# A two-branch FFN kernel on one core: its first products and first coefficient in another order

## The reference, cut to what matters

```
xn = layernorm(x)
s  = attn_ref(xn)      # 4-bit weights (16 levels x block scales) with low-rank parts, gate/up/down with silu
g  = silu(ffn_ref(xn)) # the branch below
x + s * g

# ffn_ref, HID 512, INTER 1792, three weights (w1 gate, w3 up, w2 down), each with its mean_w:
def _binary_diff_weight(w, base):
    d = w - base
    coeff = mean(abs(d))
    return base + coeff * sign(d)
h = silu(xn @ W1.T) * (xn @ W3.T);  out = h @ W2.T
```

## Time and profile before

| | |
|---|---|
| median of 3 runs | 534.47 us (534.46 to 535.68) |
| the profiled execution | 534.48 us, its span 532.7 us |
| PE busy | 519.8 us, 98% of the span, 2352 matmuls |
| DVE busy | 443.0 us, 83% |
| ACT busy | 328.5 us, 62% |
| POOL busy | 94.6 us, 18% |
| chain that ended last | PE 95%, DVE 3%, DMA 1% |
| granted PE clock | 0.999 of full |

### The profile page before, as it was taken

The page is one execution under the profiler, slowest core; times in us unless marked ns, Lnnn a source line. Parts: engine busy times, 40 slices in busy tenths (PEclk is TensorE's granted clock), DMA queues, the critical chain, the costliest instruction groups (busy, mean ns, idle before and its releaser), DMA issues.

```text
span 532.7 us, 6530 instructions
## 1 busy us (share of the span) xinstructions
PE 519.8 (98%) x2352; PEld 432.1 (81%) x2352; DVE 443.0 (83%) x520; ACT 328.5 (62%) x455; POOL 94.6 (18%) x106
## 2 busy tenths in 40 slices
PE   4999999999999999999999999999999999999997
PEld 3778888888888888888888888888888888888886
DVE  6989998988896988865898888999999898874447
ACT  2979978557546655446648557968776585464310
POOL 1311002003100310022003121300310040004491
PEclk9999999999999999999999999999999999999999
DMA  8999905045711491059228994941592387127503
GB/s 337 394 401 404 385 8 168 15 137 98 197 54 46 76 234 49 1 106 223 56 70 160 250 217 90 186 101 40 109 187 47 74 163 144 36 46 161 135 20 139
DMA packets 31745, 76.73 MB, mean 144 GB/s; under 512 B 3873, under 2 KB 7297, under 8 KB 31585
## 3 DMA queue, kind: packets, MB, share of 16 engines
q1 hardware_dynamic: 21632, 57.42, 34.4%
q0 software_dynamic: 9792, 18.88, 20.5%
q10 hardware_dynamic: 288, 0.02, 0.0%
HBM read 53.23 MB, written 2.10 MB: 104 GB/s over the span
## 4 chain that ended last, share of the span: by engine, by line
PE 95%; DVE 3%; DMA 1%; issue 0%; ACT 0%; SPq 0%
PE up_ps L1726 28%; PE gate_pair L1726 27%; PE down_pair L1767 11%; PE up_ps L1767 9%; PE down_ps L1767 7%; PE side_ps L1810 2%; PE down_pair L1726 2%; PE down_pair L1677 1%; PE up_ps L1887 1%; PE gate_pair L1887 1%; PE down_pair L1887 1%; DMA xn<-in_x 1%; PE down_pair L1849 1%; PE gate_pair L1767 1%; PE down_pair L1782 1%; DVE xn L1135 1%
## 5 line engine op out<-in xcount | busy, mean ns | idle before, releaser
L1726 PE MATMUL up_ps<-xT,gu 128*128 128x512 f32 x648 | 151.9, 390 | 0.0
L1726 PE MATMUL gate_pair<-xT,gu 128*128 128x512 f32 x624 | 148.4, 390 | 0.9 <-DVE gu L1175 0.9
L1726 PEld LDWEIGHTS up_ps<-xT,gu 128*128 128x128 f32 x648 | 121.6, 188 | 25.1
L1726 PEld LDWEIGHTS gate_pair<-xT,gu 128*128 128x128 f32 x624 | 117.2, 188 | 25.4 <-DVE gu L1175 1.4
L655 POOL DMA_DIRECT2D y<-y_part x64 | 55.4, 878 | 338.3 <-ACT y_part L819 337.1
L806 ACT ACTIVATE h<-up_ps 128x512 fp32r<-128x512 f32 x52 | 31.1, 597 | 110.1 <-DVE up_ps L1242 57.0
L865 ACT ACTIVATE ramp<-codes,bend_bias 128x1536 f32<-128x1536 uint8 x56 | 88.1, 1580 | 1.9 <-DVE acc L1350 1.6
L1350 DVE SCALAR_TENSOR_TENSOR acc<-ramp,acc 128x1536 f32<-128x1536 f32 x42 | 73.6, 1753 | 4.9 <-ACT ramp L865 4.3
L1767 PE MATMUL down_pair<-h,dn 128*128 128x512 f32 x249 | 60.9, 390 | 0.0
L1767 PEld LDWEIGHTS down_pair<-h,dn 128*128 128x128 f32 x249 | 46.8, 188 | 9.8
L1247 DVE TENSOR_TENSOR h<-up_ps,h 128x512 fp32r<-128x512 f32 x52 | 35.8, 688 | 19.7 <-ACT h L806 19.4
(11 more groups left out here) (227 smaller groups left out, 647.2 us busy)
## 6 DMA issues: line engine op xcount, KB each, us to landing
y<-y_part POOLq DMA_DIRECT2D x64, 256.0 KB, 5.1
scale<-in_scales SPq DMA_DIRECT2D x28, 384.0 KB, 5.5
scan_w<-in_w SPq DMA_DIRECT2D x15, 512.0 KB, 11.0
base<-in_mean SPq DMA_DIRECT2D x9, 768.0 KB, 4.4
scan_mean<-in_mean SPq DMA_DIRECT2D x9, 512.0 KB, 10.1
silu_gate<-in_mean SPq DMA_DIRECT2D x6, 512.0 KB, 12.4
codes<-in_codes SPq DMA_DIRECT2D x14, 192.0 KB, 6.0
xn<-in_x SPq DMA_DIRECT2D x4, 512.0 KB, 5.0
```

Source lines behind the costliest of these rows:

```text
L1726: last = nc.tensor.matmul(ps[:, :], w[:, w_part, hc * P:(hc + 1) * P], xT[:, x_part, hc, th * HALF:(th + 1) * HALF], start=(hc == 0 and w_ ...
```

## The change

The edits, all of them in the first 45 us:

- TensorE: the eighth x tile is transposed once, not three times; the 16 warm transposes that followed (`WARM_LOW`) are gone. The products with the mean weight are issued pass by pass: HI x HI and LO x HI for both token halves, then HI x LO of half 0, the signs of half 0, HI x LO of half 1, the signs of half 1. Then 5 warm transposes, the ones product (before it stood inside the second signs), 8 warm transposes, and the first weighted product (`project_split`), whose eight matmuls with the HI weight go first and the four with the LO weight last.
- `ones` holds 1/(INTER*HID), so that `side_ps` holds the coefficient itself; the halves of unit 1 are made with the column of `side_ps`, and `coeff` is a plain copy behind them (`keep_coeff`). The low part of unit 1 is made in one piece (`unit_low`), not two.
- VectorE: `x_low(0)` and `x_low(1)` go ahead of the second scan subtraction; `early_add(0)` goes behind `early_scale(1)`, `unit_low(2)` and the sixth scan subtraction.
- ScalarE: `early_high` goes ahead of the first scan signs, `scan_signs(4)` ahead of the silus of chunk 0, `unit_high(3)` ahead of `scan_signs(5)`.
- GpSimd: `early_low` no longer waits for the second scan subtraction; `unit_subtract(0)` behind it does, and `unit_subtract(1)` no longer waits for the fourth `x_low`.

The diff, without the lists whose orders stand above:

```diff
 WARM = {-1: 8, 1: 8, 3: 7}
-AGAIN = 3
-WARM_LOW = {1: 6, 2: 5, 3: 5}
+WARM_TOTAL = [5, 8]
 FIRST_TILES = 3
...
             nc.gpsimd.memset(ident[:], 0.0).then_inc(const_ready, 1)
-            nc.gpsimd.memset(ones[:], 1.0).then_inc(const_ready, 1)
+            nc.gpsimd.memset(ones[:], 1.0 / (INTER * HID)).then_inc(const_ready, 1)
             pool.wait_ge(const_ready, 2)
...
                 pool.wait_ge(gu_hi, 1)
-                pool.wait_ge(scan_diff, dve_tiles(1))
                 nc.gpsimd.tensor_tensor(gu_weight(0, GATE)[:, LO, :], unit_base(0),
...
             early_low()
+            pool.wait_ge(scan_diff, dve_tiles(1))
             unit_subtract(0)
-            pool.wait_ge(xT_lo, 4)
             unit_subtract(1)
...
             x_high(3)
+            early_high()
             scan_signs(0)
-            early_high()
             x_high(4)
...
+            def keep_coeff(m):
+                dve.wait_ge(total_ready, m + 1)
+                nc.vector.tensor_copy(coeff[:, m:m + 1], side_ps[:, m:m + 1]).then_inc(coeff_ready, 1)
...
                 dve.wait_ge(unit_sign, SPLIT_UNIT + 1)
+                dve.wait_ge(total_ready, GATE + 1)
                 nc.vector.scalar_tensor_tensor(unit_base(SPLIT_UNIT)[:, sl], unit_raw(SPLIT_UNIT)[:, sl],
-                                               coeff[:, GATE:GATE + 1], unit_base(SPLIT_UNIT)[:, sl], ALU.mult, ALU.add
+                                               side_ps[:, GATE:GATE + 1], unit_base(SPLIT_UNIT)[:, sl], ALU.mult, ALU.add
                                                ).then_inc(half_made if half == 0 else unit_made, 1)
-
-            def split_low(half):
-                sl = slice(half * HID // 2, (half + 1) * HID // 2)
-                if half == 0:
-                    dve.wait_ge(half_hi, 1)
-                else:
-                    dve.wait_ge(gu_hi, SPLIT_UNIT + 1)
-                nc.vector.tensor_tensor(unit_split(SPLIT_UNIT)[:, LO, sl], unit_base(SPLIT_UNIT)[:, sl],
-                                        unit_split(SPLIT_UNIT)[:, HI, sl].bitcast(f32), ALU.subtract
-                                        ).then_inc(half_lo if half == 0 else gu_lo, 1)
 
...
                 normalise(t)
+            x_low(0)
+            x_low(1)
             scan_subtract(1)
-            for t in range(4):
+            for t in range(2, HC):
                 x_low(t)
...
                 pe.wait_ge(xn_ready, t + 1)
-                for _ in range(AGAIN if t == TT - 1 else 1):
-                    for c in range(HC):
-                        last = nc.tensor.matmul(x_ps[t][:, c * P:(c + 1) * P], xn[:, t, c * P:(c + 1) * P], ident[:],
-                                                is_transpose=True, start=(c == 0), stop=(c == HC - 1))
+                for c in range(HC):
+                    last = nc.tensor.matmul(x_ps[t][:, c * P:(c + 1) * P], xn[:, t, c * P:(c + 1) * P], ident[:],
+                                            is_transpose=True, start=(c == 0), stop=(c == HC - 1))
                 last.then_inc(xT_tr, 1)
                 if t in (1, 3):
                     warm(side_ps, WARM[t])
-            for low, count in WARM_LOW.items():
-                pe.wait_ge(xT_lo, low)
-                warm(early_ps[0], count)
-
-            def early_mean(th):
-                pe.wait_ge(gu_lo, 1)
-                pe.wait_ge(xT_lo, TT // 2 * (th + 1))
+
+            def early_pass(th, w_part, x_part):
+                if w_part == LO:
+                    pe.wait_ge(gu_lo, 1)
+                elif x_part == LO:
+                    pe.wait_ge(xT_lo, TT // 2 * (th + 1))
+                else:
+                    pe.wait_ge(gu_hi, 1)
+                    pe.wait_ge(xT_lo, th + 1)
+                    pe.wait_ge(xT_hi, TT // 2 * (th + 1))
                 for hc in range(HC):
-                    for w_part, x_part in PASSES:
-                        nc.tensor.matmul(early_ps[th][:, :], gu_weight(0, GATE)[:, w_part, hc * P:(hc + 1) * P],
-                                         xT[:, x_part, hc, th * HALF:(th + 1) * HALF],
-                                         start=(hc == 0 and w_part == x_part == HI),
-                                         stop=(hc == HC - 1 and w_part == LO))
+                    nc.tensor.matmul(early_ps[th][:, :], gu_weight(0, GATE)[:, w_part, hc * P:(hc + 1) * P],
+                                     xT[:, x_part, hc, th * HALF:(th + 1) * HALF],
+                                     start=(hc == 0 and w_part == x_part == HI), stop=(hc == HC - 1 and x_part == LO))
 
             def early_signs(th):
                 pe.wait_ge(unit_sign, 1)
                 for hc in range(HC):
-                    if th == 1 and hc == 2:
-                        total(GATE)
                     for x_part in (HI, LO):
...
             def project(k, kind, th, total_within=None):
-                if k == SPLIT_UNIT and kind == GATE and th == 0:
-                    pe.wait_ge(half_lo, 1)
-                elif kind == GATE or k <= FIRST:
+                if kind == GATE or k <= FIRST:
                     pe.wait_ge(gu_lo, gu_count(k, kind))
...
                 for hc in range(HC):
-                    if hc == HC // 2 and k == SPLIT_UNIT and kind == GATE and th == 0:
-                        pe.wait_ge(gu_lo, gu_count(k, kind))
                     for w_part, x_part in PASSES:
...
                 last.then_inc(gate_done if kind == GATE else up_done, 1)
+
+            def project_split():
+                w = gu_weight(SPLIT_UNIT, GATE)
+                for hc in range(HC):
+                    if hc == 0:
+                        pe.wait_ge(half_hi, 1)
+                    if hc == HC // 2:
+                        pe.wait_ge(gu_hi, SPLIT_UNIT + 1)
+                    for x_part in (HI, LO):
+                        nc.tensor.matmul(gate_bank(SPLIT_UNIT, 0)[:, :], w[:, HI, hc * P:(hc + 1) * P],
+                                         xT[:, x_part, hc, 0:HALF], start=(hc == 0 and x_part == HI), stop=False)
+                pe.wait_ge(gu_lo, gu_count(SPLIT_UNIT, GATE))
+                for hc in range(HC):
+                    last = nc.tensor.matmul(gate_bank(SPLIT_UNIT, 0)[:, :], w[:, LO, hc * P:(hc + 1) * P],
+                                            xT[:, HI, hc, 0:HALF], start=False, stop=(hc == HC - 1))
+                last.then_inc(gate_done, 1)
 
...
 
-            early_mean(0)
+            for th in range(2):
+                early_pass(th, HI, HI)
+                early_pass(th, LO, HI)
+            early_pass(0, HI, LO)
             early_signs(0)
-            early_mean(1)
+            early_pass(1, HI, LO)
             early_signs(1)
-            for c in range(1, FIRST + 1):
+            warm(gate_ps[1], WARM_TOTAL[0])
+            total(GATE)
+            warm(gate_ps[1], WARM_TOTAL[1])
+            project_split()
+            project(SPLIT_UNIT, GATE, 1)
+            for c in range(SPLIT_UNIT + 1, FIRST + 1):
                 project(c, GATE, 0, UP if c == FIRST else None)
```

More of the change, by code:

```diff
@@ L362, in block_kernel @@
         half_hi = sem("half_hi")
-        half_lo = sem("half_lo")
         early_part = sem("early_part")
@@ L1001, in _ @@
             unit_signs(3)
+            scan_signs(4)
             silu(0, 0)
             silu(0, 1)
-            scan_signs(4)
             silu(1, 0)
+            unit_high(3)
             scan_signs(5)
-            unit_high(3)
             next_gate_high()
@@ L1148, in take_part @@
                                         axis=AX.X, op=ALU.add).then_inc(part_ready, 1)
+            def keep_coeff(m):
+                dve.wait_ge(total_ready, m + 1)
+                nc.vector.tensor_copy(coeff[:, m:m + 1], side_ps[:, m:m + 1]).then_inc(coeff_ready, 1)
             def take_coeff(m):
-                dve.wait_ge(total_ready, m + 1)
-                nc.vector.tensor_scalar(coeff[:, m:m + 1], side_ps[:, m:m + 1], 1.0 / (INTER * HID), None, ALU.mult
-                                        ).then_inc(coeff_ready, 1)
+                keep_coeff(m)
                 dve.wait_ge(coeff_ready, m + 1)
@@ L1536, in _ @@
             take_part(GATE)
-            take_coeff(GATE)
             split_make(0)
             split_make(1)
-            split_low(0)
-            split_low(1)
+            keep_coeff(GATE)
+            unit_low(SPLIT_UNIT)
+            dve.wait_ge(coeff_ready, 1)
             early_scale(0)
             unit_make(2)
-            early_add(0)
             early_scale(1)
             unit_low(2)
+            scan_subtract(5)
+            early_add(0)
             early_add(1)
-            scan_subtract(5)
             unit_make(3)
```

## The result

The changed kernel takes 536.16 us (median of 10 runs, 536.03 to 536.3), the kernel before 534.5 in the same comparison (10 runs, 534.32 to 535.68): ratio 1.0028, with an interval of 1.002 to 1.0036. It is slower, by 1.66 us: the interval is clear of 1, but the size is only about what the prediction took as this kernel's limit (0.3%). Forecast were 533.9 and a range up to 536.1. The first rival had 535.9. Of all executions told of here two were slow ones, one of the kernel before (886.72 us) and one of the kernel with the first meeting alone (1877.21 us), and ratios and ranges leave them out.

A forecast was written before the change was run, and what follows sets the result against it. TensorE, never waiting after 31.36, was taken as the bound. Terms -0.99 and -0.15 win 1.14 us, a wait of 0.54 at the second ones product leaves 0.6: 534.48 becomes 533.9, range 533.2 to 536.1.

The forecast's parts named there:

- The first rival: GpSimd's early low half gets in between two VectorE normalisations and later delays the sixth scan subtraction: +1.4, 535.9; chance 0.28 whole.
- The step that failed: At VectorE's four normalisations, GpSimd's early low half stays out until 17.1, is done at 18.4, and costs nothing.
- the rival's rule: At VectorE's back-to-back instructions, the memory port is given to the engine that has waited; basis of the 535.9 case.
- the whole-instruction rule: Where GpSimd and VectorE meet, whoever is first keeps the other out for a whole instruction; read from 1.72 against 1.21.
- The half version: Only the first GpSimd encounter, at the normalisations, is lost: +0.2 to +0.4, 534.8; chance 0.08.
- The start of VectorE's chain: At VectorE's third scan subtraction, less overlap with GpSimd's unit subtractions: -0.15, between 0 and -0.3.
- Early products and fillers: TensorE's 40 reordered early matmuls and changed warm transposes, before the first weighted product: moves nothing, no cost.
- From the sum to the first product: From partial sum to first weighted product: coefficient read in PSUM saves 0.50, high passes first 0.49; together -0.99.
- The price of the scalar in PSUM: In VectorE's made halves, reading the scalar operand from PSUM costs +0 to +0.3; taken as 0.
- The second ones product: Up coefficient's product: silus at 35.86 plus 13.0 of ScalarE make it start at 49.3; TensorE waits 0.54 there.
- the fourth rival: TensorE's clock falls around the ones product; the first 12 matmuls cost 2.7 more: 536.0; chance 0.04.
- the forecast case: GpSimd kept out of the normalisations, TensorE waiting 0.54 at the second ones product: gain 0.6, 533.9; chance 0.47.

The follow-up runs named there:

- the first experiment: Changed kernel with one added wait: GpSimd's early low half starts only after the last normalisation; 534.23 us, kernel before 534.42.
- e4: Kernel before, with ScalarE's high part made early and GpSimd's early low half not waiting for the scan subtraction; 535.73 us, kernel before 534.42.
- e11: Changed kernel with one added wait: GpSimd's subtraction of unit 4 waits for VectorE's sixth scan subtraction; 535.06 us, kernel before 534.43.
- e2: Changed kernel with VectorE's two early adds back at their old places, ahead of the sixth scan subtraction; 535.28 us, kernel before 534.42.
- e1: Same run as the first experiment: changed kernel, GpSimd's early low half waiting for all eight normalised tiles; 534.23 us.
- e8: Kernel of e1 plus a 128x512 GpSimd memset where the early low half had met the normalisations; one run, 534.53 us.
- e7: Changed kernel: GpSimd's early low half waits for the seventh normalisation, early adds at old places, unit 3 made before the sixth scan subtraction; 533.68 us.

## Why the prediction was wrong

**The step that failed.** "I expect GpSimd to stay out until 17.1, because the four follow each other with an overlap (0.54 busy, 0.48 apart) that leaves no gap". An overlap in the timeline is no proof against a gap. (An instruction's row also counts time in which it is held off, as the 1.51 for 0.54 shows; that the overlap of neighbours is such time would fit, but no run here shows it.) The distance was also misread: it is 1.91 divided by four, while the rows taken singly start 0.46 apart. GpSimd asked at 15.94, during the second normalisation, and the third then took 1.51. The signs that the prediction had named for it came: the four take 2.87, and the first weighted product starts after 31, at 31.34. So a way that was counted on to stay shut, at no cost, cost 0.96 us of the normalisations, and by the second meeting that came of it 1.93 us of the time. The sentence against the rival's rule was weak too: that VectorE's next instruction "read PSUM and didn't compete" said nothing for or against who would win. The 1.72 from which the whole-instruction rule was read was that of a subtraction of two tensors; a held-off normalisation is first seen here. What the rows did say, that GpSimd's work began at 34.74 before VectorE's low half had ended, pointed to the rival, and 0.28 was too little for it.

**The rival's numbers, term by term.** Normalisations +1.07 predicted, +0.96 measured; partial sum +0.93, measured +0.85; TensorE at 31.3, measured 31.34; the sixth scan subtraction at 36.2, measured 36.22; silus at 38.0, measured 38.08; ScalarE's end 50.9, measured 51.09; the ones product 51.3, measured 51.44; the time 535.9, measured 536.16. Of the last 0.26, 0.14 is there at the ones product, and 0.10 is a term that no sum had: the matmul behind it starts 0.24 after it, before 0.14 (50.03 - 49.89). The one thing it had otherwise is who stands at the second meeting: not the scan subtraction but the low half of unit 2, since it was 0.09 behind GpSimd. The delay is the same. The half version ("If only the first encounter is lost", 534.8) is the kernel without the second meeting: 535.06.

**The start of VectorE's chain**, -0.15: the third scan subtraction took 1.40 instead of 1.52, -0.12, with the meeting beside it. Right, as far as it can be told apart.

**Early products and fillers**, no cost: in the changed kernel TensorE waited 0.76 for late normalised tiles and still had to wait 0.63 for the partial sum at the ones product. Right.

**From the sum to the first product**, -0.99: measured 31.34 - 29.62 = 1.72 against 2.59, so -0.87; in the kernel before, alone, -0.85. Mis-sized by 0.12 to 0.14. The price of the scalar in PSUM, taken at 0, is not the reason: TensorE waits for the first half only, and that takes 0.49 instead of 0.48. In the changed kernel 0.08 lies ahead of it, as the half starts 0.72 behind the partial sum, where the copied coefficient had started 0.64 behind; and 0.04 lies between the half's start and the product (1.00, where the forecast's terms give 0.96). The low part was in time: no idle time between the eighth and the ninth matmul.

**The second ones product.** The chain of 13.0 from silus to the end of ScalarE: 38.08 to 51.09 is 13.01, and 36.29 to 49.29 in the first experiment is 13.0. Right. The silus at 35.86 never came about: without the first meeting they start at 36.29, 0.43 later. Of that 0.27 comes with the partial sum (28.89 against 28.77 - 0.15, the small meeting at 18.33 in it) and 0.16 behind it: here both halves count, the second made from PSUM later than from SBUF, so that ScalarE ends their high parts 0.16 later behind the sum than the forecast had it.

**The clock**, the fourth rival at 0.04: the mechanism exists, but 13 transposes keep it away, and without them the first eight matmuls cost about 1.3 more (the ninth starts at 33.67 against 32.39) and not all twelve 2.7, as the clock was back after the eight.

**What would have been the result.** Without the meeting the forecast case gives 534.23 in the first experiment, 0.2 below the kernel before and 0.3 above the 533.9. Its ones product stood at 49.65 against the 49.3 forecast, which is that difference: the halves and the small meeting at 18.33, as just told. That small meeting came with the wait I added, so the forecast case itself, GpSimd kept out without a wait, was never run.

## What to carry to other kernels

A wait that protects no data may still keep two engines apart. Before one is removed, look at when its engine will be ready now, and what runs beside it then: between back-to-back instructions of VectorE one of GpSimd that has waited can be let in, and holds the next one off until it is done. It was let in where it had come 0.32 before the end of the running one, and not where it had come 0.08 before. And a gain at the head of a kernel is worth only as much as the next hand-over has slack, here 0.44 us; to bring it to the end, the chain behind that hand-over had to be moved with it, every operation of it.

## What the hardware showed that was not expected

- Who is let in: of four back-to-back normalisations (0.54 each, 0.46 apart) one took 1.51 when GpSimd had asked at 15.94, and the four took 2.87 in each of the four kernels where it could (the changed one, e4, e11 and e2), 1.91 in those where it couldn't. Where the two rows start within 0.09 us of each other: GpSimd at 34.45 was first before VectorE at 34.54 (1.75 for 0.69); both at 34.43, VectorE was first (1.22, GpSimd's 2.37, in e1); VectorE at 34.57 was first before GpSimd at 34.59 (1.22, GpSimd's 2.35, in e8). In the last two GpSimd came 0.08 and 0.06 before VectorE's running instruction had ended, and the one queued behind that still went first. At which distance it turns over is not shown.
- A memset on GpSimd, which reads nothing, met the normalisations too: 0.28 more for the four, with the third held off until 0.28 behind the memset's end. How much of the memset's own 0.82 was waiting, this one run can't tell.
- A VectorE operation on 128x256 took 0.49 with its scalar operand in PSUM and 0.48 with it in SBUF, but the next one like it started 0.51 to 0.54 behind it instead of 0.40.
- About 2.2 us of idle time in two pieces let TensorE's clock fall to 0.50, in the profiled run, and by their times in 7 of 12; 1.8 us of transposes in the same place kept it at 1.00 in the profiled run of e7.
